# The first twelve score groups computed beside the first layer's expert units instead of after them

## The chip, the core and the metric

The kernel runs on one core of one Trainium2 chip. The metric is the device time of one execution in microseconds; for each kernel the median of its runs counts.

## What is computed

A block of three layers on x of shape 16 x 256 x 128 (4096 tokens): half a mixture-of-experts layer, causal attention, and half the same mixture-of-experts layer again, each on normalised rows and added to x.

```python
def attention(x):                      # 16 heads of 8, per sequence of 256
    Q, K, V = heads(x @ WQ), heads(x @ WK), heads(x @ WV)
    score = einsum('bhqd,bhkd->bhqk', Q, K) / sqrt(8) + causal_mask
    score = score - max(score, axis=-1)
    p = exp(score) / sum(exp(score), axis=-1)
    return einsum('bhqk,bhkd->bhqd', p, V).reshape(B, S, 128) @ WO

def experts(flat):                     # 8 experts of 256, the best 2 for each token
    combine = top2_weights(softmax(flat @ gate_w.T))
    y = einsum('neh,edh->ned', silu(flat @ w1.T) * (flat @ w3.T), w2)
    return einsum('ned,ne->nd', y, combine)

x = x + 0.5 * experts(layernorm(x))
x = x + attention(layernorm(x))
x = x + 0.5 * experts(layernorm(x))
```

## The kernel before

Every engine has a program of its own, written by hand in order; semaphores join them. The order of an engine is the order of its program.

**Units.** The expert layers run in units of one expert and 256 rows. The first layer has 16 dense units (0 to 15), then two sets of tiles of sorted rows: units 16 to 34 (`experts(0)`, 19 tiles) and 35 to 57 (`experts(1)`, 23 tiles). `U_SECOND` is 58, `LAG` is 3. A turn of the loop on TensorE is: the four down products of unit n - 3 (`down`, L1621), then twelve up products of unit n (`tile_up`, through `split_product`, L1502 to L1504) into banks 0 to 3. ScalarE copies the down result to `yb` (L841) and makes `silu` of unit n (L833); VectorE makes the `product` of unit n (L1189). SyncE (the queue SPq) loads tile k + 6 by a transposing DMA (L467) when the up products of tile k are done, then stores `yb` of tile k - 3 (L472). The loads of the second tile set start at k = 17 and k = 18 with three each, and wait for the end of its scatter. After each turn every engine calls a `beside` function (`first_groups`, with n the unit) that places other work.

**Other work beside the units.** For token group 0 and 1 (512 tokens each, two sequences) `first_step(n)` names the unit beside which TensorE transposes the normalised rows and projects Q, K and V into bank 6 (`B_M0`). SyncE stores the split Q and K in DRAM (`keep_products`, L481) and reads them back in twelve pieces as stacked rows in `zc` (`stack_row`, L487; six for heads pairs 0 to 3, counted in `zc_done[0]`, six for 4 to 7, in `zc_done[1]`). GpSimd scatters rows for the second tile set and gathers results (`gather`, L694), and VectorE adds them to x (`add`, L1198). `EARLY` is 9 tiles of the first set; three more adds are left for later.

**Attention.** A sequence is 8 head pairs. A score group (here also slot) is 8 small matmuls (`score_products`, L1734) and 4 for the mask (`score_masks`, L1751) into a pair of banks; VectorE takes the row maxima (`row_max`, L1302). After 8 of them `combine_max` joins them, GpSimd clamps (`clamp`, L725), TensorE turns them (`max_transpose`, L1782 to L1784, into bank 7), ScalarE copies (`max_copy`, L938) and SyncE places them into `zc` (`place_max`, L504), whence the transposed scores (L1764 to L1773) subtract them before the exponential (L950). A `step` is one sequence, 8 turns; each turn makes the score group of 4 positions ahead (`AHEAD` = 4). So before step 0 can start, twelve score groups are needed: 8 of sequence 0 and 4 of sequence 1. They are made after unit 57, in turns in banks 0, 1 and 2, 3. Turn 4 of step 0 is the first that reads the rows of group 1 (`zc_done[0]`).

## Time and profile before

| | |
|---|---|
| median of 3 runs | 624.39 us (619.85 to 625.75) |
| profiled execution | 619.24 us |
| its span, first to last instruction | 617.5 us |
| TensorE matmul busy | 517.3 us (84%) |
| VectorE busy | 374.3 us (61%) |
| ScalarE busy | 310.2 us (50%) |
| GpSimd busy | 267.6 us (43%) |
| mean granted TensorE clock | 0.973 |

In the rows below times are in us from the span's start, and a row of several instructions (x8) has the start of the first and the time to the end of the last. PE is TensorE, DVE VectorE, ACT ScalarE, POOL GpSimd, SPq the DMA queue of SyncE. In brackets stands how long the engine was idle before, and what ended that. Matmuls are pipelined: each has a duration of 0.27 us but the next starts 0.11 us later, so that pitches are read from starts. An fp32 matmul has two records, so the four down products of a unit are a row x8. One add is two instructions.

### The profile page before, as it was taken

How to read it: one execution, taken by the hardware profiler on the slowest of the kernel's cores; microseconds unless marked ns; L12 is line 12 of the kernel's file. 1: busy time of each engine (PE TensorE's matmuls, PEld its weight loads, DVE VectorE, ACT ScalarE, POOL GpSimd, SP SyncE). 2: the span in 40 equal slices, each digit the busy share in tenths (PEclk: the TensorE clock that was granted, in tenths of full speed). 3: DMA queues.
4: the chain of work that ended last, by engine and by line, in shares of the span. 5: the costliest groups of instructions: out<-in, count | busy, mean ns of one | idle time of the engine just before them, and what ended most of it. 6: DMA issues, size and time to landing. Idle time of an engine off the chain costs nothing.

```text
span 617.5 us, 19023 instructions
## 1 busy us (share of the span) xinstructions
PE 517.3 (84%) x7286; PEld 416.7 (67%) x7286; DVE 374.3 (61%) x995; ACT 310.2 (50%) x597; POOL 267.6 (43%) x325
## 2 busy tenths in 40 slices
PE   1779879999998578888888886777689899999995
PEld 1667858779987345555556564545368789989994
DVE  5633933333355778888989988666346343355665
ACT  4853524344334156666666765556553244345543
POOL 6865764630654033434342110554614530556562
PEclk9999988999998679999999999999989999999999
DMA  9941223546865222656212020311033546653232
GB/s 275 329 150 39 53 68 91 137 108 145 154 151 144 72 60 72 170 155 189 90 50 85 16 88 2 115 36 37 31 74 93 144 124 122 152 131 99 66 90 56
DMA packets 114662, 65.87 MB, mean 107 GB/s; under 512 B 51856, under 2 KB 108432, under 8 KB 114576
## 3 DMA queue, kind: packets, MB, share of 16 engines
q1 hardware_dynamic: 107664, 50.49, 31.1%
q0 software_dynamic: 6912, 14.17, 8.6%
q8 instruction: 62, 1.02, 0.7%
q14 instruction: 24, 0.20, 0.1%
HBM read 18.88 MB, written 34.87 MB: 87 GB/s over the span
## 4 chain that ended last, share of the span: by engine, by line
PE 37%; DVE 16%; issue 4%; ACT 3%; another core or an unknown queue 1%; DMA 1%; POOL 0%; DVEq 0%; ACTq 0%; POOLq 0%
PE bank L1621 9%; DVE negmax L1302 7%; PE bank L1502 5%; PE bank L1504 5%; PE bank L1503 5%; PE bank L1734 2%; PE bank L1797 2%; ACT pt L950 2%; PE bank L1764 2%; PE bank L1812 1%; PE bank L1751 1%; PE bank L1800 1%; DVE rden L1319 1%; PE bank L1514 1%
## 5 line engine op out<-in xcount | busy, mean ns | idle before, releaser
L1189 DVE SCALAR_TENSOR_TENSOR pt<-bank,pt 128x512 f32<-128x512 f32 x122 | 84.3, 691 | 154.5 <-PE bank L1504 72.6
L694 POOL DMA_INDIRECT yg<-sorted_y,row x108 | 104.3, 965 | 145.8 <-PE bank L1621 65.7
L950 ACT ACTIVATE pt<-bank 128x768 f32<-128x768 f32 x128 | 103.8, 811 | 88.0 <-PE bank L1773 83.1
L680 POOL DMA_INDIRECT sorted_x<-xs,row x108 | 106.2, 983 | 78.9 <-DVE pt L1189 33.0
L1621 PE MATMUL bank<-w,pt 128*128 (+1 forms) x976 | 133.1, 279 | 8.5 <-issue 7.3
L1621 PEld LDWEIGHTS bank<-w,pt 128*128 128x128 f32 x976 | 120.5, 193 | 14.1 <-issue 10.0
L1302 DVE TENSOR_REDUCE negmax<-bank 128x10 f32<-128x640 f32 x128 | 104.2, 818 | 30.2 <-PE bank L1751 26.4
L833 ACT ACTIVATE pt<-bank 128x512 f32<-128x512 f32 x122 | 73.2, 600 | 50.0 <-PE bank L1504 37.3
L841 ACT ACTIVATE yb<-bank 128x256 f32<-128x256 f32 x82 | 31.5, 384 | 76.6 <-PE bank L1621 50.7
L1734 PE MATMUL bank<-zc 63*64 63x64 f16 (+3 forms) x1024 | 44.1, 250 | 30.4 <-DVE negmax L1302 24.8
L1734 PEld LDWEIGHTS bank<-zc 63*64 63x64 f16 x1024 | 19.3, 107 | 58.1 <-DVE negmax L1302 38.7
L856 ACT ACTIVATE ot<-bank,comb 128x128 f32<-128x128 f32 x80 | 25.1, 369 | 48.2 <-PE bank L1621 24.4
L1502 PE MATMUL bank<-pt,w1h 128*128 128x256 f16 x164 | 46.2, 281 | 3.6 <-DVE logit L1082 2.6
L1764 PE MATMUL bank<-zc 64*64 64x256 f16 (+1 forms) x1024 | 44.1, 248 | 5.5 <-ACT pt L950 4.6
L1504 PE MATMUL bank<-pt,w1l 128*128 128x256 f16 x164 | 46.0, 281 | 1.9 <-issue 1.9
L1502 PE MATMUL bank<-pt,w3h 128*128 128x256 f16 x164 | 45.9, 280 | 1.4 <-issue 1.4
L1503 PE MATMUL bank<-pt,w1h 128*128 128x256 f16 x164 | 46.1, 281 | 1.0 <-issue 1.0
L1797 PE MATMUL bank<-pt,vaug 128*32 128x256 f32 x512 | 42.5, 397 | 4.9 <-issue 2.9
L1503 PE MATMUL bank<-pt,w3h 128*128 128x256 f16 x164 | 46.0, 280 | 0.7 <-issue 0.7
L1504 PE MATMUL bank<-pt,w3l 128*128 128x256 f16 x164 | 45.9, 280 | 0.3 <-issue 0.3
L1198 DVE SCALAR_TENSOR_TENSOR X<-yg,weight,X 128x128 f32<-128x128 f32 x108 | 37.7, 349 | 3.0 <-DMA yg<-sorted_y,row 1.0
L1773 PE MATMUL bank<-causal_t,ident_b 64*64 64x256 bf16 x256 | 36.0, 274 | 0.0
(171 smaller groups left out, 1022.6 us busy)
## 6 DMA issues: line engine op xcount, KB each, us to landing
sorted_y<-yb SPq DMA_DIRECT2D x82, 128.0 KB
zc<-qk_rows SPq DMA_DIRECT2D x96, 64.0 KB
sorted_x<-zeros SPq DMA_DIRECT2D x2, 2944.0 KB, 14.1
qk_rows<-qksplit SPq DMA_DIRECT2D x8, 512.0 KB
sorted_x<-zeros SPq DMA_DIRECT2D x1, 2432.0 KB, 11.5
sorted_x<-zeros SPq DMA_DIRECT2D x1, 2176.0 KB, 10.2
X<-x_in SPq DMA_DIRECT2D x8, 256.0 KB, 5.1
zc<-w_up SPq DMA_DIRECT2D x8, 256.0 KB, 6.1
```

Source lines behind the costliest of these rows:

```text
L680: ps.indirect_dma_start(out=sorted_x[s], out_offset=bass.IndirectOffsetOnAxis(ap=row[:, s, k, t:t + 1], axis=0), in_=xs[:, R0[s] + t, :], ...
L694: ps.indirect_dma_start(out=yg[:, a % D_YG, k, :], out_offset=None, in_=sorted_y[s], in_offset=bass.IndirectOffsetOnAxis(ap=row[:, s, k, t ...
L833: s_.activation(silu[:, n % D_H], bank[:, B_H1 + n % 2, :], ACT.Silu, scale=1.0 / WSCALE)\
L950: s_.activation(pt[:, hg, (u % 2) * 768:(u % 2 + 1) * 768].rearrange("p (a n) -> p a n", a=2), bank[:, B_ST:B_ST + 2, 0:384], ACT.Exp, sca ...
L1189: v_.scalar_tensor_tensor(hid[:, n % D_HID], bank[:, B_H3 + n % 2, :], 1.0 / WSCALE, silu[:, n % D_H], ALU.mult, ALU.mult).then_inc(prod_d ...
L1302: v_.tensor_reduce(negmax[:, q % 2, k, :, 0:PARTS], bank[:, b0:b0 + 2, 0:S_COLS].rearrange("p a (s k) -> p a s k", k=HALF), AX.X, ALU.max, ...
L1502: t_.matmul(dst, ah, bh, start=True, stop=False)
L1503: t_.matmul(dst, ah, bl, start=False, stop=False)
L1504: return t_.matmul(dst, al, bh, start=False, stop=True)
L1621: last = t_.matmul(y_half(n)[:, u * D:(u + 1) * D], hid[:, n % D_HID, c * SLOTS + u * P:c * SLOTS + (u + 1) * P], w2[:, bass.ds(offset + c ...
L1734: t_.matmul(bank[side(g), b0 + a, c0:c0 + keys], zc[rows, par, 0, u, q0:q0 + HALF], zc[rows, par, 1, u, e * SEQ:e * SEQ + keys], start=n = ...
L1764: t_.matmul(bank[side(g), B_ST + a, kb * SEQ:SEQ + kb * P], zc[side(a), par, 1, u, k0 + HALF * g:k0 + HALF * (g + 1)], zc[side(a), par, 0, ...
```

## The change

The twelve score groups move from behind unit 57 to the units 38 to 49, one a unit, behind the up products; all use the same pair of banks, 5 and 6 (`B_EARLY`). VectorE takes each row maximum behind the product of the unit, and joins the eight maxima of sequence 0 at unit 45; GpSimd clamps them in the middle of the gathers, TensorE turns them at unit 51 into bank 5, ScalarE copies at 52, SyncE places at tile 37. For that the work of group 0 comes earlier: normalising, transposing and projecting from units 24 to 36 to units 21 to 28, `keep_products(0, 0)` from tile 21 to 12, the twelve stack rows from tiles 24 to 35 to tiles 13 to 24. The three adds that stood among the maxima go into turns 0, 2 and 4 of step 0. Behind the units TensorE waits only for `vaug_set` and the copy of unit 57. Group 1's first transpose (unit 52) waits for the last early maximum, since bank 6 is shared.

```diff
+        FIRST_SLOT = 38
+        B_EARLY = B_T
+        MAX_TURN = FIRST_SLOT + PAIRS + AHEAD + 1
...
-            return {27: (0, 0), 30: (0, 1), 33: (0, 2), 36: (0, 3), 52: (1, 0), 54: (1, 1), 56: (1, 2)}.get(n, (None, None))
+            return {22: (0, 0), 24: (0, 1), 26: (0, 2), 28: (0, 3), 52: (1, 0), 54: (1, 1), 56: (1, 2)}.get(n, (None, None))
...
+        def early_slot(n):
+
+            return n - FIRST_SLOT if FIRST_SLOT <= n < FIRST_SLOT + PAIRS + AHEAD else None
...
             def first_groups(k):
-                if k == 21:
+                if k == 12:
                     keep_products(0, 0)
-                if k == 24:
+                if k == 13:
...
-                if 24 <= k < 36:
-                    n = k - 24
+                if 13 <= k < 25:
+                    n = k - 13
                     stack_row(0, n // 6, n // 2 % 3, n % 2)
+                if k == MAX_TURN + 2 - U_TILE[0]:
+                    place_max(0, 0)
...
             keep_products(1, 1)
-            place_max(0, 0)
...
             for t in range(RT[1]):
-                if t == 11:
+                if t == 7:
                     layer_norm(0)
...
                 gather(s, t, [k])
+                if d == 11:
+                    clamp(0, 0)
...
+                if n == MAX_TURN + 1:
+                    max_copy(0, 0, 0)
...
+                    if b == 0 and k in (0, 2, 4):
+                        add(0, EARLY + k // 2)
...
-                if n in (22, 48):
+                if n in (19, 48):
                     attention_norm(n // 48)
-                if n in (24, 50):
+                if n in (21, 50):
...
+                slot = early_slot(n)
+                if slot is not None:
+                    row_max(slot // PAIRS, slot // PAIRS, slot % PAIRS, B_EARLY)
+                if slot == PAIRS - 1:
+                    combine_max(0, 0)
...
-            for k in range(PAIRS):
-                row_max(0, 0, k, score_banks(k))
-            combine_max(0, 0)
-            for k in range(AHEAD):
-                row_max(1, 1, k, score_banks(k))
-                if k < RT[0] - EARLY:
-                    add(0, EARLY + k)
...
-                if not spare or PAIRS * b + u > spare:
-                    pe.wait_ge(s_reduced, freed(PAIRS * b + u) - spare)
+                pe.wait_ge(s_reduced, freed(PAIRS * b + u))
...
                 if which == 0:
+                    if g == 1:
+                        pe.wait_ge(s_reduced, done(PAIRS + AHEAD - 1, D_S))
                     x_transpose(g, m0_use(g))
...
+                slot = early_slot(n)
+                if slot is not None:
+                    if slot == 0:
+                        pe.wait_ge(m0_freed, m0_use(0, 3) + 1)
+                    score_products(slot // PAIRS, slot // PAIRS, slot % PAIRS, 0 if slot < PAIRS else None, B_EARLY)
+                    score_masks(B_EARLY)
+                if n == MAX_TURN:
+                    pe.wait_ge(s_reduced, done(PAIRS + AHEAD - 1, D_S))
+                    max_transpose(0, 0, 0)
...
-            for k in range(PAIRS):
-                score_products(0, 0, k, 0, score_banks(k), 1)
-                score_masks(score_banks(k))
-            for k in range(AHEAD):
-                score_products(1, 1, k, None, score_banks(k), 1)
-                score_masks(score_banks(k))
-                if k == 1:
-                    pe.wait_ge(vaug_set, 2)
-                    pe.wait_ge(y_copied, done(Y_SECOND - 1, D_Y))
-                    max_transpose(0, 0, 0)
+            pe.wait_ge(vaug_set, 2)
+            pe.wait_ge(y_copied, done(Y_SECOND - 1, D_Y))
```

How the order moves at three places. SyncE before, from the last load of the first tile set (tile 18) on: five stores follow it, then the two bunches of three loads, with no other DMA between.

```order
L467 DMA_TRANSPOSE pt<-sorted_x 128x2x256 [waits h3_ready]
L472 DMA sorted_y<-yb 128x2x128 [waits y_copied] x5
L467 DMA_TRANSPOSE pt<-sorted_x 128x2x256 [waits h3_ready,scattered1]
L467 DMA_TRANSPOSE pt<-sorted_x 128x2x256 [waits h3_ready] x2
L472 DMA sorted_y<-yb 128x2x128 [waits y_copied]
L467 DMA_TRANSPOSE pt<-sorted_x 128x2x256 [waits h3_ready] x3
L472 DMA sorted_y<-yb 128x2x128 [waits y_copied]
L467 DMA_TRANSPOSE pt<-sorted_x 128x2x256 [waits h3_ready]
```

The same place after, where lines are nine later (L476 is the load, L481 the store, L490 the store of Q and K, L496 a stack row):

```order
L476 DMA_TRANSPOSE pt<-sorted_x 128x2x256 [waits h3_ready]
L481 DMA sorted_y<-yb 128x2x128 [waits y_copied]
L490 DMA qk_rows<-qksplit 128x2048 [waits m0_freed]
L481 DMA sorted_y<-yb 128x2x128 [waits y_copied]
L496 DMA zc<-qk_rows 16x4x512 [waits qk_stored,consts,zc_set]
L481 DMA sorted_y<-yb 128x2x128 [waits y_copied]
L496 DMA zc<-qk_rows 16x4x512
L481 DMA sorted_y<-yb 128x2x128 [waits y_copied]
L496 DMA zc<-qk_rows 16x4x512
L481 DMA sorted_y<-yb 128x2x128 [waits y_copied]
L496 DMA zc<-qk_rows 16x4x512
L476 DMA_TRANSPOSE pt<-sorted_x 128x2x256 [waits h3_ready,scattered1]
```

A stack row now stands behind each of these stores, and behind the next eight.

TensorE between the up products of unit 42 and the down products of unit 40, after the change (L1516 is the last kind of up product, L1745 and L1762 are the score group, L1633 is a down product):

```order
L1516 MATMUL bank<-pt,w3l 128x256
L1745 MATMUL bank<-zc 64x64 [waits s_reduced,zc_done1]
L1745 MATMUL bank<-zc 64x128
L1745 MATMUL bank<-zc 64x64
L1745 MATMUL bank<-zc 64x128
L1745 MATMUL bank<-zc 64x256
L1745 MATMUL bank<-zc 64x192
L1745 MATMUL bank<-zc 64x256
L1745 MATMUL bank<-zc 64x192
L1762 MATMUL bank<-causal,ident_b 64x2x64 x4
L1633 ISA [waits prod_done,y_copied]
L1633 MATMUL bank<-w,pt 128x128
```

Before, the down product follows the up product directly; now slot 4's group lies between, with its waits for the maximum of slot 3 and for the second half of the stack rows.

VectorE at units 44 to 46, after the change (L1201 is the product, L1314 the row maximum, L1322 to L1324 join the eight maxima, L1210 is an add):

```order
L1201 SCALAR_TENSOR_TENSOR pt<-bank,pt 128x512 [waits silu_done,y_ready,h3_ready,x_sum]
L1314 TENSOR_REDUCE negmax<-bank 128x2x5 [waits s_ready]
L1201 SCALAR_TENSOR_TENSOR pt<-bank,pt 128x512 [waits y_ready,silu_done,h3_ready]
L1314 TENSOR_REDUCE negmax<-bank 128x2x5 [waits s_ready]
L1322 TENSOR_REDUCE negmax<-negmax 64x16 [waits s_reduced]
L1323 TENSOR_REDUCE negmax<-negmax 64x16
L1324 TENSOR_TENSOR negmax<-negmax 64x16
L1210 SCALAR_TENSOR_TENSOR X<-yg,weight,X 128x128 [waits gathered1]
L1210 SCALAR_TENSOR_TENSOR X<-yg,weight,X 128x128 [waits x_sum]
L1201 SCALAR_TENSOR_TENSOR pt<-bank,pt 128x512 [waits silu_done,y_ready,h3_ready,x_sum]
```

Before, products and adds alone stood there; each product now has a row maximum behind it, and the maximum waits for the scores of the same unit.

## Rows read from the trace of the kernel before

**Rows 1.** The page's slices: TensorE's granted clock, 40 slices of 15.4 us, in tenths.

```profile
PEclk9999988999998679999999999999989999999999
```

**Rows 2.** Windows of the seam: busy us of each engine, granted clock, DMA share, GB/s.

```profile
206.00:215.00 9.00, 4.30 (x91) 2.17 (x88) 8.59 (x17) 1.86 (x3) 0.36 (x1) 0.50 0.07 21
215.00:222.00 7.00, 5.83 (x112) 3.47 (x112) 3.81 (x12) 2.43 (x3) 3.28 (x4) 0.50 0.43 117
```

**Rows 3.** Timeline of VectorE in the seam and in turn 0 of step 0.

```profile
202.80 6.06 DVE L1302 TENSOR_REDUCE negmax<-bank 128x10 f32<-128x640 f32 x8 [2.30 <-PE bank L1751]
...
210.32 0.74 DVE L1198 SCALAR_TENSOR_TENSOR X<-yg,weight,X 128x128 f32<-128x128 f32 x2
...
215.62 0.82 DVE L1302 TENSOR_REDUCE negmax<-bank 128x10 f32<-128x640 f32 x1 [0.69 <-PE bank L1751]
...
216.37 0.86 DVE L1036 BATCH_NORM_STATS2 stats<-X 128x6 f32<-128x128 f32 x4
```

**Rows 4.** Timeline of TensorE: down products, then the score groups.

```profile
159.26 1.06 PE L1621 MATMUL bank<-w,pt 128*128 x8
...
161.46 1.06 PE L1621 MATMUL bank<-w,pt 128*128 x8
...
184.82 0.59 PE L1621 MATMUL bank<-w,pt 128*128 x3
...
192.33 1.05 PE L1621 MATMUL bank<-w,pt 128*128 x8
...
199.58 2.84 PE L1621 MATMUL bank<-w,pt 128*128 x24
...
202.35 0.33 PE L1734 MATMUL bank<-zc 63*64 63x64 f16 x8
...
202.58 0.31 PE L1734 MATMUL bank<-zc 63*64 63x64 f16 x8
...
214.98 0.48 PE L1734 MATMUL bank<-zc 63*64 63x64 f16 x8 [2.42 <-DVE negmax L1302]
...
223.06 0.33 PE L1734 MATMUL bank<-zc 63*64 63x64 f16 x8
```

**Rows 5.** Timeline of VectorE: products of units 42, 43, 51 and 57; a normalising.

```profile
117.18 1.10 DVE L1045 TENSOR_SCALAR xn<-X,meanvar,rstd 128x128 f32<-128x128 f32 x4
...
159.65 0.69 DVE L1189 SCALAR_TENSOR_TENSOR pt<-bank,pt 128x512 f32<-128x512 f32 x1 [0.36 <-ACT pt L833]
...
163.91 0.69 DVE L1189 SCALAR_TENSOR_TENSOR pt<-bank,pt 128x512 f32<-128x512 f32 x1 [3.57 <-PE bank L1621]
...
182.63 0.69 DVE L1189 SCALAR_TENSOR_TENSOR pt<-bank,pt 128x512 f32<-128x512 f32 x1 [0.95 <-issue]
...
199.81 0.69 DVE L1189 SCALAR_TENSOR_TENSOR pt<-bank,pt 128x512 f32<-128x512 f32 x1 [0.91 <-PE bank L1504]
```

**Rows 6.** Timeline of SyncE's DMA queue: loads, stack rows, stores of Q and K.

```profile
136.77 3.80 SPq L467 DMA_TRANSPOSE pt<-sorted_x  x3
...
141.25 4.49 SPq L467 DMA_TRANSPOSE pt<-sorted_x  x3
...
182.59 0.55 SPq L487 DMA_DIRECT2D zc<-qk_rows  x1
...
185.11 0.55 SPq L487 DMA_DIRECT2D zc<-qk_rows  x1
...
204.06 0.39 SPq L481 DMA_DIRECT2D qk_rows<-qksplit  x1
...
212.66 8.26 SPq L487 DMA_DIRECT2D zc<-qk_rows  x12
...
239.75 0.34 SPq L481 DMA_DIRECT2D qk_rows<-qksplit  x1
...
242.62 8.92 SPq L487 DMA_DIRECT2D zc<-qk_rows  x12
```

**Rows 7.** Timeline of ScalarE: a copy that waits for a store.

```profile
181.55 0.38 ACT L841 ACTIVATE yb<-bank 128x256 f32<-128x256 f32 x1 [2.52 <-DMA sorted_y<-yb]
```

More of the change, by code:

```diff
@@ L383, in build_macaron @@
         EARLY = 2 * TILES + 1
+        assert RT[0] - EARLY == 3
         ADD_STEPS = RT[1] // 2
@@ L407, in build_macaron @@
         AHEAD = 4
+        FIRST_SLOT = 38
+        B_EARLY = B_T
+        MAX_TURN = FIRST_SLOT + PAIRS + AHEAD + 1
+        assert MAX_TURN + 1 < U_SECOND and B_EARLY + 1 == B_M0
         def tile_of(b):
@@ L436, in build_macaron, with max_bank @@
         M1_TAIL = m1_use(batches)
+        def max_bank(use):
+            return B_M1 if use else B_EARLY
         @block.sync
@@ L697, in gather, with clamp @@
                         .then_inc(gathered[a % D_YG], 16)
+            def clamp(b, q):
+                part = negmax[:, q % 2].rearrange("p h a s -> p s (h a)")
+                hold(pool, m_combined, 3 * (b + 1))
+                ps.tensor_scalar(negmax_h[:, q % 2], part[:, 0:PARTS + 1:PARTS, :],
+                                 -MLIMIT, MLIMIT, ALU.max, ALU.min).then_inc(clamp_done, 1)
             routing_constants()
@@ L717, in _ @@
                 gather(s, t, [k])
+                if d == 11:
+                    clamp(0, 0)
                 if d == 12:
                     layer_norm(1)
-            def clamp(b, q):
-                part = negmax[:, q % 2].rearrange("p h a s -> p s (h a)")
-                hold(pool, m_combined, 3 * (b + 1))
-                ps.tensor_scalar(negmax_h[:, q % 2], part[:, 0:PARTS + 1:PARTS, :],
-                                 -MLIMIT, MLIMIT, ALU.max, ALU.min).then_inc(clamp_done, 1)
             def step(b, q, G, scores=True, ln=True, gathers=(), route=None, scatters=(None, ())):
@@ L743, in step @@
                             scatter(2, (first + n) // 2, ks=[(first + n) % 2])
-            clamp(0, 0)
             sent = 0
@@ L937, in max_copy @@
                     act.wait_ge(m_placed, 32 * (b - 1))
-                s_.activation(negmax_t[0:HEADS, q % 2, :], bank[0:HEADS, B_M1, 0:SEQ], ACT.Copy).then_inc(m1_freed, 1)
+                s_.activation(negmax_t[0:HEADS, q % 2, :], bank[0:HEADS, max_bank(use), 0:SEQ], ACT.Copy).then_inc(m1_freed, 1)
             def o_high(use):
@@ L1422, in first_groups @@
                     k_low(g, g)
[L1423 removed]
+                if n == 19:
                     dve.wait_ge(y_added, done(Y_DENSE[1] - 1, D_Y))
[L1425 removed]
+                if n in (19, 48):
                     attention_norm(n // 48)
[L1427 removed]
+                if n in (21, 50):
                     for t in range(TILES):
                         normalise(n // 50, t, TILES * ORDER[n // 50] + t)
+                slot = early_slot(n)
[3 more added lines that the diff above has]
+                    combine_max(0, 0)
                 paced_adds(0, unit)
             units(U_TILE[0] + LAG, U_SECOND, first_groups)
[L1434 to L1440 removed]
             for b in range(batches):
@@ L1717, in score_quarter, with score_products @@
                 return ((0, 0), (3, HALF))[n] if g == 0 else ((1, 0), (2, 2 * HALF))[n]
-            def score_products(b, q, u, G_z=None, b0=B_S, spare=0):
+            def score_products(b, q, u, G_z=None, b0=B_S):
                 par, e = (q // 2) % 2, q % 2
@@ L1780, in max_transpose @@
                     pe.wait_ge(m1_freed, use)
-                dst = bank[0:HEADS, B_M1, 0:SEQ]
+                dst = bank[0:HEADS, max_bank(use), 0:SEQ]
                 t_.matmul(dst[:, 0:P], negmax_h[:, q % 2, 0, :], ident_h[:, :], start=True, stop=True)
```

4 lines of the change are left out of this document (removed).

## The prediction

> **What bounds the kernel now.** I read the views from coarse to fine. The slices first: TensorE's granted clock is at 9 tenths or full nearly everywhere, and the deepest dip, 6 and 7 tenths, lies at slices 14 and 15, from 201 to 232 us [rows 1]. That is the seam between the first layer's tiles and the attention. The windows show what the seam is: from 206 to 215 us TensorE is busy 4.30 of 9.00 us and VectorE 8.59, and the clock is at 0.50, which is the 1.2 GHz level; it is still 0.50 from 215 to 222 us [rows 2]. So the seam is bound by VectorE, one row maximum after the other (8 in 6.06 us, then adds of 0.74 us between further ones) [rows 3]. On TensorE the first score group stands at 202.35 and the first turn of step 0, the thirteenth group, at 214.98: 12.6 us of seam [rows 4].
>
> Ahead of the seam TensorE is the bound: a unit's four down products start at 159.26 and the next unit's at 161.46, a pitch of 2.20 us [rows 4]. But the products on VectorE come slower, unit 42 at 159.65 and unit 51 at 182.63: 22.98 / 9 = 2.55 us a unit [rows 5]. That is the pitch of SyncE's queue while it also issues the stack rows, one at 182.59 and the next at 185.11: 2.52 us [rows 6]. ScalarE shows how it reaches the others: a copy waits 2.52 us for an earlier store of `yb` [rows 7]. TensorE pays this back at 184.82, where the next unit's down products start only at 192.33, 7.5 us for a turn of 2.2 [rows 4]: the stretch loses 5.3 us there.
>
> **The change, part by part.** I count on the profiled execution's own times, and ask how much earlier the fifth turn of step 0 (its score group at 223.06 [rows 4]) begins. After it both kernels do the same.
>
> *The seam goes.* Step 0 waits only for the copy of unit 57, for which the last down products (three units, 24 records) start at 199.58 and take 2.84 us [rows 4]; with the copy, step 0 can start at about 202.9. Clamp, turn and placing of the first maxima lie beside the units and cost the seam nothing: GpSimd's clamp, ScalarE's copy and SyncE's two small DMAs stand between work of engines that wait for TensorE there.
>
> *Then a new wait is next.* The fifth turn reads the second group's stack rows. Their source is stored at 204.06 [rows 6], in both kernels just behind the last tile store. Before, the rows started at 212.66, since they queue behind the placing of the maxima; now nothing holds them but the store itself. Its nearest case is in the attention: store at 239.75, first row at 242.62, 2.87 us [rows 6]. The first six of twelve rows take half of 8.26 us, 4.13, and the last must land: between 0 and the 2.87 us of the larger transfer, I take 1.2, nearer to a small one. 204.06 + 2.87 + 4.13 + 1.2 = 212.3. Without that wait VectorE sets the four turns. The three adds of 0.74 us now lie in them: 2.4 us for turn 0 (maximum 0.82, add 0.74, statistics 0.86) [rows 3], then about 1.5 each (maximum, add or small pieces), so near 209.8. The wait costs 2.5 us and hides the adds. The fifth turn moves from 223.06 to 212.3: **10.8 us earlier, if the units end when they did.**
>
> *Twelve slots inside units.* Two groups directly behind each other start at 202.35 and 202.58, 0.23 us at the full clock [rows 4]. TensorE has no idle time in the pitch of 2.20, so all of it counts: 12 x 0.23 + 0.2 for the turned maxima = 3.0. Upper bound: twice that per group, 0.45, if entering and leaving such small tiles is not free, 5.6.
>
> *The stack rows of group 0, eleven turns of SyncE's queue earlier.* Two effects. The rows now share the queue with the two bunches of three loads, which start at 136.77 (the second layer set's scatter ends then) and take 3.80 and 4.49 us [rows 6]. With 0.6 for each store and each row: 136.77 + 3.80 + 1.2 + 4.49 + 1.2 = 147.5, where the sixth row is out. Landed at 148.7, it is in time for slot 0, which TensorE reaches at 159.26 - 4 x 2.20 = 150.5. Six more turns of 2.52 us: the twelfth row is out at 162.6, landed at 163.8. Slot 4 needs it and TensorE stands there at 159.26 + 4 x 0.23 = 160.2. **It waits 3.6 us** (0 if the queue runs its other pitch, 6 if the rows land late). Queued behind it on TensorE is the whole of unit 43. Gain: from then on the queue is free of rows and runs at less than TensorE's pitch, so what it cost, 5.3 us, can come back. I take 3.5 of it; the gathers stay, and one of the stalls may be no matter of this queue. Bounds 0 and 5.3.
>
> *VectorE within a unit.* A slot's scores wait for the maximum of the slot before, because there is only one pair of banks. That maximum (0.82) stands behind the product (0.69). In a pitch of 2.43 this leaves 0.9 us. Unit 43's product starts at 163.91, 2.4 us after its last up matmul, which ended where the down products start at 161.46 [rows 4, 5]. So late products can now stop TensorE, which before ran two units ahead. I take 1.0, bounds 0 and 4.
>
> *Projections of group 0, five to eight units earlier.* The same matmuls, so nothing, except that the normalised tile is needed one unit after it is made instead of three. The normalising takes 1.10 us [rows 5] behind a product of 0.69; if that product is as late as unit 43's, 2.4 us, less the 2.2 of the unit between, TensorE waits some 2 us. Bounds 0 and 3; products here need not be late, and I take 0.5.
>
> *The clock.* Before, the four turns ran at the 1.2 GHz level. After, they may start at 2.4 GHz, but the wait of 2.5 us is a light stretch such as that in which it fell. I take 1.2 us for some turns at the low level, bounds 0 and 2.
>
> **The sum.** 10.8 - 3.0 - 3.6 + 3.5 - 1.0 - 0.5 - 1.2 = **5.0 us**. The profiled execution took 619.24, of which 617.5 are its span; so 614.2 in its terms. It lies 5.15 below the median of the runs, and I take the saving from the median: 624.39 - 5.0 = **619.4 us**. That is 0.8%, and below about 1% a measurement of this kernel hardly tells a change from none.
>
> **The rivals.**
> *The queue is given back whole, and no wait replaces the seam.* If slot 4's rows are in time or nearly (wait 1 instead of 3.6), the relief is 5.3, and the clock stays up, the sum is 10.8 - 3.0 - 1 + 5.3 - 0.5 - 0 - 0 = 11.6: 612.8 us. For it: the pitch of 2.52 equals that of the products. Against it: two bunches of loads ahead of the rows. A gain over 1% needs only part of this: 0.37.
>
> *The pair of banks chains TensorE to VectorE.* Place: units 43 to 49. If the products stay as late as they were, each excess over 0.9 us is paid. Unit 43 pays 1.5 [rows 4, 5]; seven units of about that are 9 to 10 us, and the relief is 0, for the stores are still what delays. 10.8 - 3.0 - 3.6 - 9.5 - 0.5 - 1.2 = -7.0: 631.4 us. It decides from the point where chain and unrelieved stores take over 6.0 us beyond the slots and slot 4's wait. Against it: a stop of TensorE takes the lead away that makes the next product late, so excesses hardly add up. 0.12 for all slower by over 1%.
>
> *Entering and leaving small tiles costs.* Row to row I see none: the 24 records from 199.58, each 0.11 us behind the other, have their last start near 202.2, and the scores start at 202.35 [rows 4]. The way back is not shown. At the upper bound of 5.6 for the slots the sum falls to 2.4: 622.0 us. 0.1, within the forecast's class. The Trainium skill speaks for it, and against this change: TensorEngine Tiling (Array Packing), Key Properties, says that a change of tiling mode, not just of tile, drains TensorE. TensorE: Matmul & The Clock Gate, Part 2, puts the end of a lone matmul at some 0.175 us; by an estimate from that page, 24 changes would cost 4.2 us and leave 0.8. The trace does not agree for the way in.
>
> That the slots do not move is no rival: the order of each engine shows all twelve beside units 38 to 49.
>
> **How the numbers follow.** Forecast and small-tile rival lie within 1%: 0.51 together. Over 1% faster 0.37, over 1% slower 0.12. The low end, 612, takes the first rival nearly whole; at the high end, 627, relief is missing and half of the chain is paid. The runs shown spread from 619.85 to 625.75, which adds a little at both ends.
>
> **What would show it.** Step 0's first score group stands 0.3 us behind the last down products, with no row maxima of slots 0 to 11 there; the granted clock over the seam is above 0.5. The stack row group's twelfth row is issued near 162, and TensorE waits at slot 4, not at slot 0. SyncE's queue idles between rows from 165 on, and products of units 45 to 57 come at 2.2 to 2.5. Unit 57's product, 199.81 before [rows 5], comes near 204.5. The fifth turn of step 0 waits for the second group's rows. Wrong it would be if unit 57 came later than 209 (the chain), or before 201 (the first rival), or if the attention from the fifth turn on took another time than before, for which I see no reason.

## The result, and the profile after

The changed kernel takes 629.2 us (median of 15 runs, 624.41 to 634.32) where the kernel before, measured beside it, takes 621.98 (15 runs, 619.85 to 626.66). The ratio on record, which compares only runs in the chip's faster state and so leaves out the 634.32, is 1.0085, with a 95% interval of 1.0057 to 1.0113: **slower by 0.9%**, where 0.8% faster was forecast. It is not the quotient of the two medians, which is 1.0116; here and below the two differ by up to 0.3%. The two profiled executions agree with that: 624.41 and 619.24 us.

The slices of the page, TensorE's granted clock in tenths, to be held against [rows 1]: the dip of the seam at slices 14 and 15 is still there, and a second one stands before it, at slice 11 (156 to 171 us).

```profile
PEclk9999989899799869999999999898899999999998
```

The timeline of TensorE after the change, lines 11 or 12 later than in [rows 4] (L1745 begins a score group, L1633 are the down products, L1514 to L1516 the up products).

```profile
151.56 0.27 PE L1516 MATMUL bank<-pt,w3l 128*128 128x256 f16 x1
151.76 0.33 PE L1745 MATMUL bank<-zc 63*64 63x64 f16 x8
...
152.08 1.16 PE L1633 MATMUL bank<-w,pt 128*128 x8
153.07 0.27 PE L1514 MATMUL bank<-pt,w1h 128*128 128x256 f16 x1
...
154.48 0.33 PE L1745 MATMUL bank<-zc 63*64 63x64 f16 x8
...
166.56 0.48 PE L1745 MATMUL bank<-zc 63*64 63x64 f16 x8 [5.96 <-DMA zc<-qk_rows]
...
208.23 2.84 PE L1633 MATMUL bank<-w,pt 128*128 x24
211.59 0.33 PE L1745 MATMUL bank<-zc 63*64 63x64 f16 x8 [0.52 <-issue]
...
222.72 0.48 PE L1745 MATMUL bank<-zc 63*64 63x64 f16 x8 [2.53 <-DMA zc<-qk_rows]
```

Three things are to be seen. A unit with a slot has a pitch of 154.48 - 151.76 = 2.72 us, 0.52 over the 2.20 of [rows 4]. At slot 4 (166.56) TensorE has waited 5.96 us for a stack row. And step 0 starts where the prediction has it, behind the last down products, with no seam; but its fifth turn is at 222.72, only 0.34 us ahead of the 223.06 of [rows 4].

The timeline of SyncE's queue, to be held against [rows 6]:

```profile
146.57 0.54 SPq L496 DMA_DIRECT2D zc<-qk_rows  x1
...
163.43 0.54 SPq L496 DMA_DIRECT2D zc<-qk_rows  x1
...
212.01 0.38 SPq L490 DMA_DIRECT2D qk_rows<-qksplit  x1
216.57 8.30 SPq L496 DMA_DIRECT2D zc<-qk_rows  x12
```

The sixth row stands at 146.57 and the twelfth at 163.43; forecast were 147.5 and 162.6. But TensorE goes on only 3.13 us after the twelfth is issued. The rows of group 1 start 4.56 us behind their store, not 2.87. Windows around both waits (columns as in [rows 2]) show what they do to the clock: 0.50, the 1.2 GHz level, at slot 4, and again up to 228 us, while before the clock was at 0.50 from 206 to 222.

```profile
164.00:168.00 4.00, 1.44 (x16) 1.21 (x17) 1.49 (x2) 0.00 (x0) 0.18 (x1) 0.50 0.69 167
216.00:220.00 4.00, 4.00 (x60) 2.52 (x52) 1.97 (x4) 1.27 (x2) 3.19 (x4) 0.50 0.33 85
...
224.00:228.00 4.00, 4.00 (x63) 2.67 (x61) 3.35 (x10) 2.48 (x5) 2.05 (x2) 0.50 0.28 84
```

Two products of VectorE, of units 42 and 57 (unit 57's was at 199.81 in [rows 5], and near 204.5 in the forecast):

```profile
165.01 0.69 DVE L1201 SCALAR_TENSOR_TENSOR pt<-bank,pt 128x512 f32<-128x512 f32 x1 [5.26 <-remote]
...
208.69 0.69 DVE L1201 SCALAR_TENSOR_TENSOR pt<-bank,pt 128x512 f32<-128x512 f32 x1
```

So the units end 8.9 us later, the way from there to the fifth turn is 9.2 us shorter (14.03 us, 23.25 before), and 0.3 us is left. From here on the changed kernel loses again: it is 2.2 us behind at the start of step 2 and 5.1 at the end (spans of 622.6 and 617.5). The low clock up to 228 us and one more add in turn 4 (see g3) can account for the first part; what makes the rest is not shown.

### The profile page after: what moved, and what is told of

The parts are those of the page before. It is cut to its first block, busy times and chain, and to the rows that moved or that the text cites. A ratio compares the mean times of both kernels' runs of the same rounds, so it can differ in the third digit from the quotient of the medians.

```text
span 622.6 us, 19024 instructions
## 1 busy us (share of the span) xinstructions
PE 521.8 (84%) x7286; PEld 420.5 (68%) x7286; DVE 373.5 (60%) x995; ACT 310.3 (50%) x597; POOL 267.5 (43%) x325
## 4 chain that ended last, share of the span: by engine, by line
PE 38%; DVE 16%; issue 4%; ACT 3%; another core or an unknown queue 1%; DVEq 0%; ACTq 0%
PE bank L1633 9%; DVE negmax L1314 7%; PE bank L1514 5%; PE bank L1515 5%; PE bank L1516 5%; PE bank L1745 2%; PE bank L1808 2%; PE bank L1823 2%; PE bank L1775 2%; PE bank L1762 2%; ACT pt L961 1%; PE bank L1811 1%; DVE r_xn L1082 1%; PE bank L1526 1%; DVE rden L1331 1%
## 5 line engine op out<-in xcount | busy, mean ns | idle before, releaser
L1201 DVE SCALAR_TENSOR_TENSOR pt<-bank,pt 128x512 f32<-128x512 f32 x122 | 84.3, 691 | 152.0 <-PE bank L1516 60.1
L1633 PE MATMUL bank<-w,pt 128*128 (+1 forms) x976 | 134.2, 280 | 7.6 <-issue 7.2
L1633 PEld LDWEIGHTS bank<-w,pt 128*128 128x128 f32 x976 | 121.1, 194 | 14.8 <-issue 11.2
L1314 DVE TENSOR_REDUCE negmax<-bank 128x10 f32<-128x640 f32 x128 | 104.5, 817 | 38.3 <-PE bank L1762 32.4
L1745 PE MATMUL bank<-zc 63*64 63x64 f16 (+3 forms) x1024 | 44.2, 250 | 34.6 <-DVE negmax L1314 20.6
L1745 PEld LDWEIGHTS bank<-zc 63*64 63x64 f16 x1024 | 19.2, 107 | 63.3 <-DVE negmax L1314 32.7
L1775 PE MATMUL bank<-zc 64*64 64x256 f16 (+1 forms) x1024 | 45.7, 255 | 4.0 <-ACT pt L961 3.6
L1514 PE MATMUL bank<-pt,w1h 128*128 128x256 f16 x164 | 46.1, 281 | 3.3 <-DVE logit L1094 2.7
L1514 PE MATMUL bank<-pt,w3h 128*128 128x256 f16 x164 | 45.7, 279 | 0.9 <-issue 0.9
L1516 PE MATMUL bank<-pt,w1l 128*128 128x256 f16 x164 | 46.0, 281 | 0.4 <-issue 0.4
L1516 PE MATMUL bank<-pt,w3l 128*128 128x256 f16 x164 | 45.7, 279 | 0.0
L1210 DVE SCALAR_TENSOR_TENSOR X<-yg,weight,X 128x128 f32<-128x128 f32 x108 | 37.6, 348 | 2.3 <-DMA yg<-sorted_y,row 0.3
```

The lines of the kernel that those rows point to most:

```text
L1201: v_.scalar_tensor_tensor(hid[:, n % D_HID], bank[:, B_H3 + n % 2, :], 1.0 / WSCALE, silu[:, n % D_H], ALU.mult, ALU.mult).then_inc(prod_d ...
L1314: v_.tensor_reduce(negmax[:, q % 2, k, :, 0:PARTS], bank[:, b0:b0 + 2, 0:S_COLS].rearrange("p a (s k) -> p a s k", k=HALF), AX.X, ALU.max, ...
L1514: t_.matmul(dst, ah, bh, start=True, stop=False)
L1516: return t_.matmul(dst, al, bh, start=False, stop=True)
L1633: last = t_.matmul(y_half(n)[:, u * D:(u + 1) * D], hid[:, n % D_HID, c * SLOTS + u * P:c * SLOTS + (u + 1) * P], w2[:, bass.ds(offset + c ...
L1745: t_.matmul(bank[side(g), b0 + a, c0:c0 + keys], zc[rows, par, 0, u, q0:q0 + HALF], zc[rows, par, 1, u, e * SEQ:e * SEQ + keys], start=n = ...
```

## The experiments

Each set of runs was made on one chip, with the kernel before timed beside it, so a ratio holds within its set; a comparison of ratios from two sets is weaker. The changed kernel itself was measured first and in the third set (g1) only. The medians of before were 618.1 (first set), 618.4 (second), 570.5 (third), 624.3 (fourth) and 622.7 us (fifth). In the third set every kernel is some 50 us faster, which proved of use. The record gives the chips the numbers 8, 15, 8, 14 and 0: whether the first and the third set ran on two chips with one number, or on one chip at two speeds, it does not say.

| kernel | set | us | ratio to before | 95% |
|---|---|---|---|---|
| e1: group 0 early, slots in the seam | 1 | 625.79 | 1.0144 | 1.0095 to 1.0193 |
| again | 4 | 628.17 | 1.0085 | 1.0051 to 1.0120 |
| again | 5 | 630.09 | 1.0112 | 1.0065 to 1.0160 |
| e2: changed kernel, slots from unit 40 | 1 | 622.97 | 1.0094 | 1.0057 to 1.0130 |
| e3: changed kernel, group 0's rows by ScalarE | 1 | 616.32 | 0.9985 | 0.9957 to 1.0014 |
| again | 4 | 621.26 | 0.9964 | 0.9932 to 0.9996 |
| e4: changed kernel, score groups twice | 1 | 626.17 | 1.0120 | 1.0071 to 1.0169 |
| f1: before, group 0's rows by ScalarE | 2 | 617.05 | 1.0009 | 0.9976 to 1.0042 |
| f2: e1, group 0's rows by ScalarE | 2 | 622.44 | 1.0057 | 1.0021 to 1.0092 |
| f3: e3, all two units earlier | 2 | 616.23 | 0.9974 | 0.9944 to 1.0005 |
| f4: before, projections early | 2 | 623.99 | 1.0105 | 1.0056 to 1.0154 |
| again | 4 | 627.49 | 1.0048 | 1.0019 to 1.0077 |
| again | 5 | 628.49 | 1.0103 | 1.0050 to 1.0157 |
| g1: changed kernel again | 3 | 577.56 | 1.0103 | 1.0070 to 1.0137 |
| g2: projections early, late rows by ScalarE | 3 | 570.55 | 0.9999 | 0.9977 to 1.0022 |
| g3: f3, group 1's store ahead of three tiles | 3 | 564.93 | 0.9900 | 0.9860 to 0.9940 |
| again | 4 | 616.44 | 0.9866 | 0.9829 to 0.9904 |

**e1, only group 0's work early.** The kernel before with the projections at units 22 to 28 (and the normalising ahead of them), the store at tile 12 and the rows from tile 13.

```diff
-            return {27: (0, 0), 30: (0, 1), 33: (0, 2), 36: (0, 3), 52: (1, 0), ...
+            return {22: (0, 0), 24: (0, 1), 26: (0, 2), 28: (0, 3), 52: (1, 0), ...
...
-                if k == 21:
+                if k == 12:
                     keep_products(0, 0)
...
-                if 24 <= k < 36:
-                    n = k - 24
+                if 13 <= k < 25:
+                    n = k - 13
...
```

> Only the work of group 0 is early (projections, store of Q and K, stack rows), the twelve score groups stay in the seam. Theory A (the wait for the stack rows at slot 4, 6.0 us in the trace of the changed kernel, and the low clock behind it cost the gain): nothing waits for the rows here, and the queue of SyncE is free of them from 165 us on, so the 5.3 us that TensorE loses near 185 us before come back; 617 to 619 us, 3 to 5 below before. Rival B (the early group 0 work by itself costs time, by its order on the queues): 622 us or more, and unit 57 later than before's 199.8.

1.0144, and 1.0085 and 1.0112 in its repeats: the part of the change that should give back up to 5.3 us loses by itself about as much as the whole change (1.0085 and 1.0103). Whether moving the slots on top of it gains anything, these ratios of different sets do not tell.

**e2, the slots two units later** (`FIRST_SLOT = 40`).

> The changed kernel with the score groups at units 40 to 51 instead of 38 to 49. Slot 4 is reached some 5 us later, the rows land at the same time. Theory A: the wait there falls from 6.0 to about 1 us and the clock stays at its high level: 6 to 7 us faster than the changed kernel, near before (621 to 623). Rival C (what the groups cost within the units is the loss, 0.52 us each, and the wait only takes over what the queue would have cost anyway): within 1.5 us of the changed kernel.

1.0094, where the changed kernel has 1.0085 and 1.0103 in other sets: the 6 to 7 us of theory A are not there, although slot 4 waits for no row here. Part of the reason may be its fifth turn, which waits 3.69 us for a row instead of 2.53. And at about the same time another wait stands, at the slot before. VectorE reaches the maximum that the slot needs only at 166.90, and the row puts down no local cause for its 3.33 us ("remote"); ScalarE has 4.88 us of the same kind:

```profile
167.78 0.33 PE L1745 MATMUL bank<-zc 63*64 63x64 f16 x8 [3.02 <-DVE negmax L1314]
```

```profile
162.88 0.69 DVE L1201 SCALAR_TENSOR_TENSOR pt<-bank,pt 128x512 f32<-128x512 f32 x1 [1.07 <-issue]
166.90 0.82 DVE L1314 TENSOR_REDUCE negmax<-bank 128x10 f32<-128x640 f32 x1 [3.33 <-remote]
```

```profile
167.67 0.38 ACT L852 ACTIVATE yb<-bank 128x256 f32<-128x256 f32 x1 [4.88 <-remote]
```

The first trace of the changed kernel has this too: while TensorE waited for the row, the product of unit 42 was held for 5.26 us, "remote", until 165.01. So outside the third set the row wait takes over, in part, time that is lost there in another way without it; how much is not shown.

**e3, group 0's rows on ScalarE's DMA queue.** The changed kernel with the twelve rows taken off SyncE's queue.

```diff
-                if 13 <= k < 25:
-                    n = k - 13
-                    stack_row(0, n // 6, n // 2 % 3, n % 2)
...
+                if 30 <= n < 36:
+                    for m in (2 * (n - 30), 2 * (n - 30) + 1):
+                        half, r, sd = m // 6, m // 2 % 3, m % 2
...
+                        s_.dma_start(zc[r:P:8, 0, sd, prs, :], src[:, part, prs, :]).then_inc(zc_done[half], 16)
```

> The changed kernel with group 0's twelve stack rows issued from ScalarE's DMA queue, two beside each of units 30 to 35, none on SyncE's. Theory A: no wait at slot 4, no low clock behind it, SyncE's queue at 1.9 us a tile throughout: 7 to 9 us faster than the changed kernel, 620 to 622. Rival D (the DMA engines, not the queue that issues, are what makes the rows late): wait at slot 4 stays above 3 us, less than 3 us gained.

0.9985, and 0.9964 in its second measurement: 1.0% and 1.2% under the changed kernel's 1.0085, which is of another set. The wait at slot 4 is gone from the trace and most units with slots keep their 2.72 us. What stays is the wait at the fifth turn, 2.52 us here.

```profile
159.85 0.33 PE L1748 MATMUL bank<-zc 63*64 63x64 f16 x8
163.21 0.33 PE L1748 MATMUL bank<-zc 63*64 63x64 f16 x8 [0.58 <-issue]
165.93 0.33 PE L1748 MATMUL bank<-zc 63*64 63x64 f16 x8
...
217.61 0.48 PE L1748 MATMUL bank<-zc 63*64 63x64 f16 x8 [2.52 <-DMA zc<-qk_rows]
```

The second measurement, with 3.65 us at the fifth turn, is within its expectation:

> The changed kernel with group 0's rows on ScalarE's queue (0.9985 in its first measurement). By the second profiles of before and of the changed kernel, the wait at the fifth slot with what follows at the low clock costs 8 us, the wait for group 1's rows 4 to 5: so this kernel gains 7 to 8 us on the changed kernel and still waits at the fifth turn for 2.5 to 5 us; ratio 0.996 to 1.000.

**e4, the price of a slot.** The changed kernel with each early score group issued twice; the second writes the same scores over the first.

```diff
                     score_products(slot // PAIRS, slot // PAIRS, slot % PAIRS, 0 if slot < PAIRS else None, B_EARLY)
+                    score_masks(B_EARLY, False)
+                    score_products(slot // PAIRS, slot // PAIRS, slot % PAIRS, 0 if slot < PAIRS else None, B_EARLY)
                     score_masks(B_EARLY)
```

> The changed kernel with each of the twelve early score groups (8 products, 4 masks) issued twice in a row into the same banks, so TensorE computes each group twice. Slots 0 to 3 lie ahead of the wait at slot 4, which absorbs them; 8 slots count. If the 0.52 us of a slot is 0.23 of matmuls and the rest the change between 128 x 128 and 64 x 64 tiles, the second copy costs 0.23 each: 2 us slower than the changed kernel, and the pitch of slots 5 to 10 goes from 2.72 to 2.95. If a group of this form costs 0.52 wherever it stands: 4 us slower and a pitch of 3.24.

```profile
154.58 0.33 PE L1745 MATMUL bank<-zc 63*64 63x64 f16 x8
154.80 0.31 PE L1745 MATMUL bank<-zc 63*64 63x64 f16 x8
157.50 0.33 PE L1745 MATMUL bank<-zc 63*64 63x64 f16 x8
```

The second group starts 0.22 us behind the first, and the pitch is 2.92, 0.20 over 2.72. So a group by itself costs 0.20 to 0.23, and the first one in a unit 0.52: some 0.3 us is for going from 128x128 tiles to 64x64 ones and back. That is the small-tile rival, and a little over the 5.6 us of its upper bound (12 x 0.52 = 6.2). The time, 1.0120, fits the expected 2 us, but with four runs and in another set than the changed kernel it could not decide between the two cases; the pitch does. The Trainium skill (TensorEngine Tiling (Array Packing), Key Properties) says that such a change of mode drains TensorE; the trace agrees, and shows where the cost falls. On the way in the group starts 151.76 - 151.56 = 0.20 us behind the last up product, where another up product would start after 0.11. Another 0.10 is on the way back: the first up product starts 153.07 - 152.08 = 0.99 behind the first down product; in a unit without a slot it is 2.20 less twelve up products of 0.11, or 0.89.

**f1, the relief by itself.** The kernel before, unchanged but for its twelve rows, which ScalarE's queue issues beside units 40 to 45.

> The kernel before with one thing changed: the twelve stack rows of group 0 are issued by ScalarE's DMA queue, two beside each of units 40 to 45, and not by SyncE's; slots, projections and all else stay. Before spends 2.52 us per tile on SyncE's queue while the rows are on it (160 to 191 us). Theory Q (the rows on SyncE's queue cost time wherever they stand, about what the run with early rows on ScalarE's queue won over the changed kernel, 1%): ratio 0.988 to 0.993, the group's first score slot 4 to 7 us earlier than 202.35. Theory R (the queue only costs when the rows come early, beside the loads that are still ahead of their units; at before's place it is hidden, and the starved stretch at 186 to 188 us has another cause): ratio 0.998 to 1.002.

1.0009; the interval, down to 0.9976, leaves room for a gain of 1.5 us and not for 3.5. SyncE's queue no longer runs at 2.52 us a tile there, and nothing is won. TensorE still loses time at about the same place, at 182.7 to 184.1 us of that trace. In the third set the stretch from product 37 to 57 takes 46.11 us with late rows on SyncE's queue (g4) and 45.79 with late rows on ScalarE's (g2). **The relief that the prediction counted at 3.5 us does not exist**, but for some tenths at most.

**f2, e1 without the rows on SyncE's queue**, and **f4, only the projections early**:

> The run with only group 0's work early (1.0144), but its twelve rows issued by ScalarE's DMA queue beside units 30 to 35; the slots are in the seam. Against the run that has the same rows and the slots in the units (0.9985) it tells what the slots are worth once no row is waited for; against the run with only group 0's work early it tells what the queue costs. Theory Q: the queue costs 8 to 9 us, so 0.998 to 1.002, and the slots in the units gain or lose under 2 us beside it. Theory S (the slots in the units are worth what the prediction's sum said without its wait, 10.8 less 12 x 0.52 = 4.6 us): 1.006 against before, 0.7% over the run with slots in the units. If the early projections themselves are the cost: 1.012 or more.

> The kernel before with only group 0's layer norm, transposes and projections at units 22 to 28; the store of its products and its twelve rows stay on SyncE's queue where before has them, slots in the seam. With the rows early as well it was 1.0144. Theory Q (the rows' place on the queue is the cost): 0.998 to 1.002. Theory of the engines (eight units of 2.2 us with projections, while TensorE's work ahead is short, is the cost): 1.010 to 1.015.

f2 is at 1.0057, under all three measurements of e1 (by 0.3 to 0.9%, in other sets), and f4 at 1.0105. So early projections cost something without any early row, which the prediction had at 0.5 us. The last pair is f2 and e3: the slots in the units are worth 0.7%, 4.5 us, when no row is waited for at slot 4. That is near 10.8 - 12 x 0.52 = 4.6, but each of the two ratios, of different sets, is known only to some 0.3%.

**g2, the projections early and late rows on ScalarE's queue**, in the third set:

> Group 0's projections at units 22 to 28, the store of its products where before has it, its twelve rows on ScalarE's queue beside units 40 to 45, slots in the seam. Measured so far, against before: late projections and late rows on ScalarE's queue 1.0009, early projections and late rows on SyncE's 1.0105, early projections and early rows on ScalarE's 1.0057. If early projections are a cost of their own: 1.005 to 1.010. If it was the early rows in the third and SyncE's queue in the second: 0.999 to 1.003.

0.9999. Either the place of the rows or the chip and its speed make the difference to f4. Repeats of e1 and f4 were to tell.

> The kernel before with group 0's projections, the store of its products and its rows early, on SyncE's queue, slots in the seam (1.0144 in its first measurement). If the early work costs by itself: 1.010 to 1.018 again. If that was starved stretches, which differ from layout to layout and from chip to chip: 0.998 to 1.004 on a chip whose trace of before shows none.

> The kernel before with only group 0's layer norm and projections early; store and rows on SyncE's queue where before has them (1.0105 in its first measurement, six runs). If early projections cost by themselves 1.008 to 1.012; if not, 0.998 to 1.002, as with the rows on ScalarE's queue (0.9999).

> Group 0's projections, store and rows early on SyncE's queue, slots in the seam, third measurement. On a chip without starved stretches 0.998 to 1.004 if these were the cost, 1.008 or more if the work itself is; on a chip with them 1.008 to 1.014 by either.

> Only group 0's projections early, third measurement. On a chip without starved stretches 0.998 to 1.002 if these were the cost; on a chip with them 1.004 to 1.010.

None of them met the third set's speed (before at 624.3 and 622.7 us). They confirm a loss at this speed: 0.5 to 1.05% for the projections alone, 0.85 to 1.4% with store and rows. The first repeats, 1.0085 and 1.0048, lie between the two cases that were expected for each. What this loss consists of is not shown (see the last section).

**g1 and g4, changed kernel and kernel before once more.**

> The changed kernel once more, unaltered, on the chip of the experiments, with a second profile. Its first profiled execution was the fastest of its 15 and before's was above its median, so that the two traces end at the same time (624.41 and 624.39) while the medians differ by 7 us. If the ratio of 1.0085 belongs to the kernels: 1.006 to 1.012 here too, and the second trace shows the wait for the seventh row at slot 4 again at 5 to 7 us and the slots 2.72 us apart. If it belongs to the chip of the first measurement: 1.000 to 1.003.

> The kernel before once more, unaltered, for a second profile on this chip. The places where TensorE starves with nothing shown as the cause: if they belong to the program, the second trace has them at the same matmuls (the 293rd, 438th, 684th and 1220th) and of about the same length; if they are chance, elsewhere.

The first expectation has one number wrong: 624.39 is the median of the first three runs of before; its profiled execution took 619.24. g1 came out at 1.0103, so the loss belongs to the kernel. In this set neither trace has a stretch in which TensorE starves without a cause shown, so the pair can be compared stretch by stretch. Products on VectorE, then exponentials on ScalarE (turns 0 and 4), first of g4 (before), then of g1 (changed):

```profile
53.59 0.69 DVE L1189 SCALAR_TENSOR_TENSOR pt<-bank,pt 128x512 f32<-128x512 f32 x1 [1.18 <-PE bank L1504]
...
128.32 0.69 DVE L1189 SCALAR_TENSOR_TENSOR pt<-bank,pt 128x512 f32<-128x512 f32 x1 [2.23 <-PE bank L1504]
...
174.43 0.69 DVE L1189 SCALAR_TENSOR_TENSOR pt<-bank,pt 128x512 f32<-128x512 f32 x1
...
190.72 0.81 ACT L950 ACTIVATE pt<-bank 128x768 f32<-128x768 f32 x1 [3.77 <-PE bank L1773]
...
197.96 0.81 ACT L950 ACTIVATE pt<-bank 128x768 f32<-128x768 f32 x1
```

```profile
56.15 0.69 DVE L1201 SCALAR_TENSOR_TENSOR pt<-bank,pt 128x512 f32<-128x512 f32 x1 [1.18 <-PE bank L1516]
...
129.94 0.69 DVE L1201 SCALAR_TENSOR_TENSOR pt<-bank,pt 128x512 f32<-128x512 f32 x1 [1.51 <-PE bank L1516]
...
143.20 0.69 DVE L1201 SCALAR_TENSOR_TENSOR pt<-bank,pt 128x512 f32<-128x512 f32 x1 [1.25 <-PE bank L1516]
153.93 0.69 DVE L1201 SCALAR_TENSOR_TENSOR pt<-bank,pt 128x512 f32<-128x512 f32 x1 [3.73 <-PE bank L1516]
...
191.00 0.69 DVE L1201 SCALAR_TENSOR_TENSOR pt<-bank,pt 128x512 f32<-128x512 f32 x1 [0.91 <-PE bank L1516]
...
195.46 0.79 ACT L961 ACTIVATE pt<-bank 128x768 f32<-128x768 f32 x1
...
206.86 0.81 ACT L961 ACTIVATE pt<-bank 128x768 f32<-128x768 f32 x1 [5.61 <-PE bank L1784]
```

The units are 5, 37, 57 (and 42 and 43 in g1). The differences between such rows:

| stretch | before | changed | difference |
|---|---|---|---|
| product 5 to 37 (projections early) | 74.73 | 73.79 | -0.94 |
| product 37 to 57 (slots, wait) | 46.11 | 61.06 | +14.95 |
| product 57 to turn 0 (seam) | 16.29 | 4.46 | -11.83 |
| turn 0 to turn 4 | 7.24 | 11.40 | +4.16 |
| turn 4 to 8 | 7.00 | 7.88 | +0.88 |

The sum is 7.2, and the medians differ by 7.1. The two profiled executions are 9.75 us apart (578.49 and 568.74); 2.56 of that stand before product 5, where both kernels run the same program, and behind turn 8 the changed one is 0.3 us quicker. The first row also says that in this set early projections cost nothing. The 14.95 are 6.2 for twelve slots, 8.0 at slot 4 (products 42 and 43 are 10.73 us apart, 2.21 before, less the slot's 0.52) and 0.7 more. The 8.0 are the wait and the low clock behind it, on TensorE of g1:

```profile
148.73 0.48 PE L1745 MATMUL bank<-zc 63*64 63x64 f16 x8 [5.60 <-DMA zc<-qk_rows]
149.25 2.08 PE L1633 MATMUL bank<-w,pt 128*128 x8
153.82 0.48 PE L1745 MATMUL bank<-zc 63*64 63x64 f16 x8
...
205.63 0.48 PE L1745 MATMUL bank<-zc 63*64 63x64 f16 x8 [5.01 <-DMA zc<-qk_rows]
```

The unit after slot 4 takes 153.82 - 148.73 = 5.09 us instead of 2.72, with the eight down products at 2.08 instead of 1.16: another 2.4 us for a wait of 5.6. The last row is the wait at the fifth turn.

**f3 and g3, both waits away.** f3 is e3 with slots (from unit 36) and group 1's layer norm and projections (50, 52, 54) two units earlier; g3 also puts the store of group 1's products ahead of the last three tiles' stores:

```diff
-        FIRST_SLOT = 38
+        FIRST_SLOT = 36
-            ... 52: (1, 0), 54: (1, 1), 56: (1, 2)}
+            ... 50: (1, 0), 52: (1, 1), 54: (1, 2)}
+                if k == U_SECOND - U_TILE[0] - 1:
+                    keep_products(1, 1)
...
-            keep_products(1, 1)
```

> The kernel with group 0's rows on ScalarE's queue (0.9985), with slots (first at unit 36), group 1's layer norm, transposes and projections (50, 52, 54) all two units earlier. In that run the fifth turn of step 0 waited 2.52 us for group 1's rows, whose store began at 206.90, and the clock was low in turns 2 to 5. If that wait is what is left of the seam: the store at about 202, no wait at the fifth turn, 2.5 to 4 us less, ratio 0.992 to 0.995. If the store only waits for SyncE's queue (seven stores of y rows stand between 196.6 and 206.9): the same time, 0.998 to 1.0.

> The run with everything two units earlier (0.9974), and with the store of group 1's products put ahead of the last three stores of y rows on SyncE's queue (in that run it was issued at 205.46, behind nine such stores, and the fifth turn waited 2.89 us for the rows). If that wait is all that is left there: the store at 198 to 200, rows from 205.5, no wait at the fifth turn, 2.5 to 3.5 us less than that run, ratio 0.992 to 0.995. If later stores of y rows, and the gathers behind them, take its place: 0.997 to 1.0.

> Everything two units earlier, group 0's rows on ScalarE's queue, group 1's products stored ahead of the last three tiles (0.990 in its first measurement, six runs): 0.986 to 0.994 again, 2.5 to 5 us under the run with the wait at the fifth turn.

f3 gave 0.9974, near the second of its two cases (0.998 to 1.0), and by its mechanism: its store was still issued only at 205.46, behind nine stores of y rows, and the fifth turn waited 2.89 us. g3 gave **0.990 and 0.9866, the one version that clearly beats both kernels** (e3's 0.9964 is under 1 by a hair). SyncE's queue and TensorE in g3, third set:

```profile
179.74 0.39 SPq L490 DMA_DIRECT2D qk_rows<-qksplit  x1
181.46 2.15 SPq L481 DMA_DIRECT2D sorted_y<-yb  x3
183.72 8.89 SPq L496 DMA_DIRECT2D zc<-qk_rows  x12
```

```profile
183.32 0.33 PE L1749 MATMUL bank<-zc 63*64 63x64 f16 x8 [0.52 <-issue]
...
191.10 0.33 PE L1749 MATMUL bank<-zc 63*64 63x64 f16 x8
```

The rows start 3.98 us behind the store, but now that time lies beside the last tiles, and the fifth turn (191.10) waits for nothing. In the stretches of the table above g3 has 74.61, 51.97, 4.45, 7.23 and 7.82: against before -0.12, +5.86 (the slots), -11.84, -0.01 and +0.82. The last, as large as g1's 0.88, comes here without a wait ahead of it and at the full clock (1.00 in the window). VectorE has hardly any idle time in turns 4 to 8 and does one add more there, the third of those that came out of the seam:

```profile
192.43 0.74 DVE L1214 SCALAR_TENSOR_TENSOR X<-yg,weight,X 128x128 f32<-128x128 f32 x2
```

```profile
192.00:200.00 8.00, 5.38 (x147) 3.49 (x151) 6.97 (x16) 4.76 (x8) 2.28 (x4) 1.00 0.18 47
```

## Why the prediction was wrong

- **The relief of SyncE's queue (+3.5) is the step that failed in kind.** A queue pitch of 2.52 us equal to the products' pitch was taken for the cause of the 5.3 us lost at 184.8. f1 takes the rows off the queue and wins nothing; in the third set the kernel before (g4) has that pitch, 2.54 us, and its products 37 to 57 come at 46.11 / 20 = 2.31 us, with no such loss:

```profile
163.01 0.55 SPq L487 DMA_DIRECT2D zc<-qk_rows  x1
...
165.55 0.55 SPq L487 DMA_DIRECT2D zc<-qk_rows  x1
```

The 5.3 us are a stretch with no cause shown, of which rows say "issue" (last section). And not all of them were lost: 0.75 us, from 191.58 to 192.33, are three matmuls on another tile (`xh`, `xl`), which only some units have.

- **The wait at slot 4 (-3.6) was right in place and too small.** The issue time of the twelfth row was forecast within 1 us, but such a row takes 3.13 us until TensorE goes on, not 1.2. It was 5.96 and 5.60 us, near the bound of 6, and with the low clock behind it, which the prediction had counted for the seam alone, 8.0 in the third set. At 4.4 us more than forecast it is the largest single error of the sum. At the first set's speed e2, without this wait, shows no gain; with the rows off SyncE's queue (e3) the gain is 1.0 to 1.2%.
- **The slots (-3.0) cost 6.2**, 0.52 each; the small-tile rival was right, and this error alone would not have turned the sign. Its "row to row I see none" came from a rounded reading: in the trace before, too, the first group starts 0.20 us behind the last down product (202.15), where the next would come after 0.11.
- **The fifth turn at 212.3** was reckoned from a store at 204.06, although the same sum moves the units later. The store goes with the units (212.01), its rows start 4.56 us behind it and not 2.87, and the row's landing counts again: 222.72. This is the end of the chain, and a delay of the units is paid in full there. The wait counted at 2.5 us in the sum measured 2.53 in the first trace, and 5.01 in the third set.
- **The seam (part of the 10.8)** was right: 11.8 us between product 57 and turn 0.
- **The bank pair (-1.0)** was small, 0.7 us at most in g1 (in the first trace slots waited 0.55 and 0.40 us for a maximum); that rival is out, although its time, 631.4, came near the one measured. **Early projections (-0.5)** cost nothing in the third set, and in the others 0.5 to 1.05%, 3 to 6.5 us. **"After the fifth turn both kernels do the same"** misses 0.9 us: the third of the moved adds, 0.74 us, stands in turn 4 on the busy VectorE (g3).

With the measured terms of g1 the sum is 11.8 - 6.2 - 8.0 - 0.7 + 0.9 - 4.2 - 0.9 = -7.3, and from the unrounded ones -7.2, where the forecast had +5.0. These are the table's rows once more, so that they add up proves nothing; which wait or change each stands for is what e3, e4, f3 and g3 show.

## What to carry to other kernels

When work moves out of a visible gap into a full stretch, what it reads must be ready earlier by the same amount: here taking the gap away gained 11.8 us, and two late transfers took 12.2 back (8.0 and 4.2). Each was cured by where its DMAs are issued (another engine's queue; ahead of three stores), not by moving less. Two equal pitches are no proof that one causes the other; taking the suspect off its queue costs one run. And a time that a sum takes from before must move with the terms of the same sum.

## What the hardware showed that was not expected

**Stretches in which TensorE starves.** The timeline of the kernel before at the loss discussed above; eight down products that take 1.06 us elsewhere take 4.4, and the last row is the first of the three further matmuls:

```profile
184.82 0.59 PE L1621 MATMUL bank<-w,pt 128*128 x3
186.28 0.27 PE L1621 MATMUL bank<-w,pt 128*128 x1 [0.86 <-issue]
187.00 0.37 PE L1621 MATMUL bank<-w,pt 128*128 x1 [0.45 <-issue]
188.42 0.81 PE L1621 MATMUL bank<-w,pt 128*128 x3 [1.05 <-issue]
...
191.58 0.48 PE L1502 MATMUL bank<-xh,wsh 128*128 128x512 f16 x1
```

Such stretches, of 0.6 to 4.9 us in sum, lie in the traces of the first measurement and of sets 1, 2, 4 and 5, and they come back at nearly the same counts of matmuls: at the 294th in 14 of the 16 traces, at the 428th to 444th in all, and at the 599th to 615th with early projections or at the 684th and 693rd without. At the 1,020th to 1,065th ten of the 14 traces with early projections have one of some 0.6 us or more, and neither of the two without. Near the 1,210th all those with slots in the seam but the first of e1 have one, and the changed kernel has none. Added up over a whole trace, TensorE's idle time put down to "issue" is 17 to 28 us in these 16 and 0.5 to 1.3 us in the four of the third set (g1 to g4), where no such stretch is found and where the kernels are 48 to 54 us faster than the same ones elsewhere.

So the places belong to the program, and whether they starve depends on something that differs between the sets. Whether that is the chip is not shown, since sets 1 and 3 bear the same chip number. What the stretches are stays open: no DMA or semaphore of the traces stands against them. The load of the DMA engines alone does not make one. Its share was 0.91 at 184 to 186 us before, where TensorE starves, and 0.82 at 164 to 166 us of g4, around the same 1,220th matmul, where it does not. That early projections cost 0.5 to 1.05% only in sets that show such stretches fits. But g2 also differs from f4 in the rows' queue, and neither e1 nor f4 was run in the third set, so that this is the cause was not shown.
